# A DLRM tower on one core: MLP layers in 64-row matmul pieces over two PSUM banks, ScalarE's sums straight to SBUF, and one PSUM copy moved to ScalarE

## The reference

```python
e = stack([tbl_f[ids[:, f]] for f in range(32)], axis=1)      # 1024 x 32 x 64
p, q = e[:, ROW_IDX], e[:, COL_IDX]                           # the 496 pairs i < j
z = einsum('bne,hne,bnh->bn', p, kernel, q)                   # kernel: 64 x 496 x 64
h = concatenate([z, dense_ctx], axis=1)                       # 1024 x 512
h = maximum(h @ W_top1 + b_top1, 0)                           # 512 -> 512
h = maximum(h @ W_top2 + b_top2, 0)                           # 512 -> 256
y = h @ W_top3                                                # 256 -> 1
```

## Time and profile before

| | |
|---|---|
| median of 3 runs | 402.61 us (401.84 to 402.92) |
| the profiled execution | 402.61 us, its span 400.8 us |
| TensorE matmul busy | 371.6 us, 93% of the span |
| VectorE busy | 354.9 us, 89% |
| ScalarE busy | 315.4 us, 79% |
| GpSimd busy | 241.8 us, 60% |
| mean granted TensorE clock | 0.987 |

### The profile page before, as it was taken

How to read it: one execution, slowest core, us unless ns; L and a number is a source line. 1 busy time by engine, 2 the same in 40 slices (tenths; PEclk the granted TensorE clock), 3 DMA queues, 4 the chain that set the end, 5 groups by cost and what they waited for, 6 DMA issues and landing times.

```text
span 400.8 us, 13206 instructions
## 1 busy us (share of the span) xinstructions
PE 371.6 (93%) x4464; PEld 277.7 (69%) x4464; DVE 354.9 (89%) x512; ACT 315.4 (79%) x2887; POOL 241.8 (60%) x260
## 2 busy tenths in 40 slices
PE   0468889899999999999999999999999999999987
PEld 0244657587777877678777877778777877778666
DVE  0249999899999999999999999999999999999971
ACT  1157696897969987898869987798869988798862
POOL 5677777766666666676676666666666666640000
PEclk9968999999999999999999999999999999999999
DMA  3566792111111111111111111111111111110000
GB/s 82 173 196 198 226 262 41 26 27 24 26 26 24 25 25 27 23 28 26 25 27 24 25 25 24 29 25 26 24 25 26 25 28 23 25 21 3 2 2 2
DMA packets 14563, 19.25 MB, mean 48 GB/s; under 512 B 7192, under 2 KB 7840, under 8 KB 14496
## 3 DMA queue, kind: packets, MB, share of 16 engines
q0 software_dynamic: 8192, 8.40, 11.2%
q1 hardware_dynamic: 6304, 10.00, 7.9%
HBM read 18.39 MB, written 0.00 MB: 46 GB/s over the span
## 4 chain that ended last, share of the span: by engine, by line
PE 84%; DVE 5%; POOL 4%; issue 3%; DMA 2%; ACT 1%; DVEq 0%
PE u_ps L570 28%; PE u_ps L577 26%; PE side_ps L591 14%; PE side_ps L625 7%; POOL emb L363 4%; PE side_ps L636 3%; PE u_ps L555 2%; DVE prod_s L502 2%; DVE prod_t L484 2%; DMA emb<-tbl,ids_sb 2%; ACT prod_s L404 1%; PE u_ps L657 1%; PE side_ps L649 1%; PE side_ps L617 1%; DVE emb_t L471 1%
## 5 line engine op out<-in xcount | busy, mean ns | idle before, releaser
L404 ACT ACTIVATE prod_s<-prod_s 128x64 f32<-128x64 f32 x1408 | 293.0, 372 | 77.1 <-DVE prod_s L502 76.6
L363 POOL DMA_INDIRECT emb<-tbl,ids_sb x256 | 241.6, 944 | 114.6 <-issue 35.4
L404 ACT ACTIVATION_READ_ACCUMULATOR prod_s<-prod_s 128x1 f32 x1408 | 277.2, 287 | 0.0
L484 DVE TENSOR_TENSOR prod_t<-u_ps,emb_t 128x1024 f32<-128x1024 f32 x128 | 155.7, 1217 | 8.0 <-PE u_ps L570 7.3
L502 DVE TENSOR_TENSOR prod_s<-u_ps,emb 128x512 f32<-128x512 f32 (+4 forms) x224 | 151.2, 721 | 11.1 <-PE u_ps L577 10.5
L570 PEld LDWEIGHTS u_ps<-emb_t,k_sb 64*128 64x128 f32 x2048 | 129.2, 190 | 36.8 <-DVE prod_s L502 12.8
L570 PE MATMUL u_ps<-emb_t,k_sb 64*128 64x128 f32 x2048 | 139.5, 279 | 3.3 <-DVE emb_t L471 1.5
L577 PE MATMUL u_ps<-k_sb,emb_t 64*128 64x512 f32 (+5 forms) x704 | 128.0, 483 | 3.7 <-DVE emb_t L471 2.1
L577 PEld LDWEIGHTS u_ps<-k_sb,emb_t 64*128 64x128 f32 x704 | 63.2, 192 | 26.9 <-issue 11.3
L591 PE MATMUL side_ps<-prod_t,pick_sb 128*32 128x256 f32 x1024 | 63.3, 382 | 0.0
L511 DVE TENSOR_REDUCE h<-prod_s 128x4 f32<-128x256 f32 x128 | 52.4, 409 | 0.0
(11 more groups left out here) (23 smaller groups left out, 38.3 us busy)
## 6 DMA issues: line engine op xcount, KB each, us to landing
k_sb<-k_pairs SPq DMA_DIRECT2D x9, 512.0 KB, 4.0
emb<-tbl,ids_sb POOLq DMA_INDIRECT x256, 2.5
k_sb<-k_pairs SPq DMA_DIRECT2D x6, 480.0 KB, 4.6
w_sb<-w SPq DMA_DIRECT2D x1, 1024.0 KB
w_sb<-w SPq DMA_DIRECT2D x1, 512.0 KB
k_sb<-k_pairs SPq DMA_DIRECT2D x1, 448.0 KB, 3.9
h<-dense SPq DMA_DIRECT2D x8, 8.0 KB
out<-y_row SPq DMA_DIRECT2D x8, 0.5 KB
```

Source lines behind the costliest of these rows:

```text
L363: nc.gpsimd.indirect_dma_start(emb[t % EMBS][:, f * EMBED:(f + 1) * EMBED], None, tables[f], bass.IndirectOffsetOnAxis(ap=ids_sb[:, t, f:f ...
L404: done = nc.scalar.activation(slot, slot, ACT.Copy, accum_out=acc_ps[:, t % 2, column:column + 1])
L484: done = nc.vector.tensor_tensor(prod_t[at % TRING][:].rearrange("p (h x) -> p h x", h=HALVES), u, low.unsqueeze(1).to_broadcast([P, HALVE ...
```

## The change

Five things are edited together.

1. **The hidden layers in 64-row pieces.** `layer` does half of the work of a pair of outputs in one piece: row half 0 of the array works on one output, row half 1 on the other, with two different banks (`side_ps` and the new `hidden_ps`), over the four chunks of the input. The second piece (phase 1) swaps the halves and so completes both sums; it waits until the first piece is complete. The first layer is four pieces after blocks 7, 9, 10 and 12, the second layer two after blocks 17 and 18.
2. **Sums straight to SBUF.** ScalarE's `accum_out` points to `h0[t]` in SBUF. `acc_ps` and `copy_acc` go; its bank becomes `hidden_ps`.
3. **Part 0 is copied by ScalarE.** For tiles 2 to 7 the copy of the turned part 0 is done by ScalarE (at 26 in its order, so between its sums of blocks 25 and 27), with a semaphore of its own, `emb_turned`.
4. **Positions.** Turns after blocks 4 and 11 instead of 3 and 12; `late_spread` after block 4 instead of 3, with five picks instead of four; ScalarE's `copy_spread` stands after its sums of block 1 instead of 2; `hidden1`'s relu after 12 (at 13), as before behind the sums of block 10; the logit and picks 0 to 3 after block 22 instead of 23, three picks after block 31 instead of four; the logit is copied at 30 instead of 23.
5. **Gathers.** The entries that waited for MLP steps wait for blocks 12, 18 and 8. The order string is written as one string and is the same.

```diff
-    ("u", 9), ("u", 10), ("u", 12), ("mlp", 2), ("u", 13), ("u", 14), ("u", 15), ("u", 17), ("u", 18), ("mlp", 3),
+    ("u", 9), ("u", 10), ("u", 12), ("u", 12), ("u", 13), ("u", 14), ("u", 15), ("u", 17), ("u", 18), ("u", 18),
...
-    ("u", 0), ("u", 1), ("u", 3), ("pick", 15), ("u", 4), ("u", 5), ("u", 6), ("u", 8), ("mlp", 0)]
+    ("u", 0), ("u", 1), ("u", 3), ("pick", 15), ("u", 4), ("u", 5), ("u", 6), ("u", 8), ("u", 8)]
...
-TURN_AT = {3: 1, 12: 2}
+TURN_AT = {4: 1, 11: 2}
...
+COPY_EARLY_AT = 26
+
+def on_act(kind, t, part):
+
+    return kind == "turn" and t > 1 and part == 0
...
-PORTION = NT // 4
-LATE_SPREAD_AT, HIDDEN1_AT, LATE_HIDDEN1_AT, HIDDEN2_AT, SUMS_AT, LATE_SUMS_AT, SPREAD_AT = 3, 8, 12, 18, 23, 27, 31
-LAST_SPREAD_AT = 29
+LATE_SPREAD_AT, SPREAD_COPY_AT = 4, 1
+PORTIONS = {22: (0, 4), 27: (4, 8), 31: (8, 11)}
+LAST_PORTIONS = {22: (0, 4), 27: (4, 8), 29: (8, 11)}
+SUMS_AT = min(PORTIONS)
+LATE = max(stop for _, stop in PORTIONS.values())
+LOGIT_COPY_AT = 30
+HIDDEN1 = {7: (0, 0), 9: (0, 1), 10: (1, 0), 12: (1, 1)}
+HIDDEN2 = {17: 0, 18: 1}
+HIDDEN1_COPY_AT, HIDDEN2_COPY_AT = 13, 18
...
-        acc_ps = ctx.enter_context(nc.psum_tensor("acc_ps", [P, 2, 2 * P], F32))
+        hidden_ps = ctx.enter_context(nc.psum_tensor("hidden_ps", [P, 4, P], F32))
+        mlp_ps = [side_ps, hidden_ps]
...
-                    done = nc.scalar.activation(slot, slot, ACT.Copy, accum_out=acc_ps[:, t % 2, column:column + 1])
+                    done = nc.scalar.activation(slot, slot, ACT.Copy, accum_out=h0[t][:, column:column + 1])
...
-            def copy_acc(t):
-                act.wait_ge(summed_a, (t + 1) * NS)
-                nc.scalar.activation(h0[t][:, :ON_ACT], acc_ps[:, t % 2, :ON_ACT], ACT.Copy).then_inc(acc_copied, 1)
+            def copy_turned(t, part):
+                act.wait_ge(slot_filled, filled("turn", t, part))
+                first, last = parts_of(t)[part]
+
+                at = SLOT_USE["turn", t, part]
+                turned_half = u_ps[at % USLOTS][:].rearrange("p (h m b) -> p m h b", h=HALVES, b=P // 2)
+                nc.scalar.activation(emb_t[t % 2][:, first:last, :].rearrange("p m (h b) -> p m h b", h=HALVES),
+                                     turned_half[:, :last - first], ACT.Copy).then_inc(emb_turned, 1)
...
+            def layer(to, weights, x, phase, m0, m1):
+
+                for c in range(4):
+                    for half, m in enumerate((m1, m0) if phase else (m0, m1)):
+                        rows = slice(half * P // 2, (half + 1) * P // 2)
+                        done = nc.tensor.matmul(to[m], weights[rows, c, m * P:(m + 1) * P], x[rows, c],
+                                                start=(phase == 0 and c == 0), stop=(phase == 1 and c == 3))
+                return done
+
+            def hidden1(t, pair, phase):
+                part = 2 * pair + phase
+                if part == 0:
                     pe.wait_ge(side_copied, STEPS * t + 1)
...
+                else:
+                    pe.wait_ge(layer_part, LAYER_PARTS * t + part)
+                to = [mlp_ps[m // 2][:, m % 2] for m in range(4)]
+                layer(to, w1_sb, h0_t, phase, pair, pair + 2).then_inc(mlp_mm if part == 3 else layer_part, 1)
+
+            def hidden2(t, phase):
+                if phase == 0:
+                    pe.wait_ge(side_copied, STEPS * t + 2)
+                else:
+                    pe.wait_ge(layer_part, LAYER_PARTS * (t + 1))
+                layer([mlp_ps[m][:, 0] for m in range(2)], w2_sb, h1_t, phase, 0, 1,
+                      ).then_inc(mlp_mm if phase else layer_part, 1)
...
-            pick_sums(last, 3 * PORTION, NT - 1)
+            pick_sums(last, LATE, NT - 1)
+            pe.wait_ge(y_copied, last)
             spread_straight(last, spread_ps).then_inc(last_turned, 1)
```

More of the change, by code:

```diff
@@ L233, in slot_uses, with filled, turn_of @@
     return uses
-SLOT_USE = {use: at for at, use in enumerate(slot_uses())}
-def used(t, n):
[L241 to L249, removed]
-PORTION = NT // 4
-LATE_SPREAD_AT, HIDDEN1_AT, LATE_HIDDEN1_AT, HIDDEN2_AT, SUMS_AT, LATE_SUMS_AT, SPREAD_AT = 3, 8, 12, 18, 23, 27, 31
-LAST_SPREAD_AT = 29
-PICKS_AT = [SUMS_AT, LATE_SUMS_AT, SPREAD_AT, LATE_SPREAD_AT]
-MLP_STEPS_AT = [HIDDEN1_AT, HIDDEN1_AT, LATE_HIDDEN1_AT, HIDDEN2_AT]
+SLOT_USES = slot_uses()
+SLOT_USE = {use: at for at, use in enumerate(SLOT_USES)}
+COPY_EARLY_AT = 26
+def on_act(kind, t, part):
+    return kind == "turn" and t > 1 and part == 0
+EMPTIED = {}
+for use in SLOT_USES:
+    EMPTIED[use] = 1 + sum(on_act(*other) == on_act(*use) for other in EMPTIED)
+def filled(kind, t, at):
+    return SLOT_USE[kind, t, at] + 1
+def used(t, n):
+    return EMPTIED["u", t, n]
+def turn_of(t, n):
+    return "turn", t, part_of(parts_of(t), n)
+assert all(SLOT_USE[turn_of(t, n)] < SLOT_USE["u", t, n] for t in range(TILES) for n in range(NB))
+LATE_SPREAD_AT, SPREAD_COPY_AT = 4, 1
[7 more added lines that the diff above has]
+HIDDEN1_COPY_AT, HIDDEN2_COPY_AT = 13, 18
 STEPS = 3
-LOGIT = CHUNKS - 1
+LOGIT = 3
+LAYER_PARTS = 4
 def build(nc, ids, tables, k_pairs, dense, w1, b1, w2, b2, w3, ident, pick, out):
@@ L466, in copy_turned @@
                 at = SLOT_USE["turn", t, part]
-                dve.wait_ge(slot_filled, at + 1)
+                dve.wait_ge(slot_filled, filled("turn", t, part))
                 first, last = parts_of(t)[part]
@@ L521, in _ @@
                         copy_turned(t, own_turns(t)[n])
-                    if early_turn(t, n):
+                    if early_turn(t, n) and not on_act("turn", t + 1, 0):
                         copy_turned(t + 1, 0)
@@ L537, in _, with emptied @@
         def _(pe):
+            def emptied(use):
+                pe.wait_ge(emb_turned if on_act(*use) else slot_emptied, EMPTIED[use])
             def slot_free(at):
                 if at >= USLOTS:
-                    pe.wait_ge(slot_emptied, at - USLOTS + 1)
+                    emptied(SLOT_USES[at - USLOTS])
                 return u_ps[at % USLOTS]
@@ L560, in block_u @@
             def block_u(t, n):
-                pe.wait_ge(slot_emptied, turned(t, n))
+                emptied(turn_of(t, n))
                 u = slot_free(SLOT_USE["u", t, n])
@@ L618, in spread_straight @@
                 return done
-            def hidden1(t, portion):
-                if portion == 0:
-                    pe.wait_ge(side_copied, STEPS * t + 1)
-                for m in range(2 * portion, 2 * portion + 2):
-                    for c in range(4):
-                        done = nc.tensor.matmul(side_ps[:, m], w1_sb[:, c, m * P:(m + 1) * P], h0_t[:, c],
-                                                start=(c == 0), stop=(c == 3))
-                    if m == 3:
-                        done.then_inc(mlp_mm, 1)
-                    else:
-                        done.then_inc(mlp_step, 1)
@@ L632, in hidden2 @@
-            def hidden2(t):
-                pe.wait_ge(side_copied, STEPS * t + 2)
-                for m in range(2):
-                    for c in range(4):
-                        done = nc.tensor.matmul(side_ps[:, m], w2_sb[:, c, m * P:(m + 1) * P], h1_t[:, c],
-                                                start=(c == 0), stop=(c == 3))
-                    if m == 1:
-                        done.then_inc(mlp_mm, 1)
-                    else:
-                        done.then_inc(mlp_step, 1)
+            def layer(to, weights, x, phase, m0, m1):
[5 more added lines that the diff above has]
+                return done
```

77 lines of the change are left out of this document (31 added, 46 removed).

## The result

The changed kernel took 415.48 us, median of four runs (412.62 to 416.56), against 402.62 us (401.84 to 402.92) for the kernel before on the same chip: 1.031 times as long, 95% interval 1.026 to 1.037. The forecast was 393.8 us and faster. Its profiled execution took 415.1 us, its span is 413.3.

A forecast was written before the change was run, and what follows sets the result against it. TensorE was taken to bound the 45.39 us tile period, VectorE only 1.27 us behind. Six tiles at 1.20 us plus 2.0 at the end, less 0.4 of new waits, saves 8.8: 402.6 to 393.8 us, range 391 to 400.

The forecast's parts named there:

- Sums straight to SBUF: ScalarE's 176 sums a tile: SBUF adds at most 0.06 us a pair, taken as 0, so still 0.197 us.
- The first rival: ScalarE's sums get slower, TensorE waits for the relu before the second layer: 406 us at 30 ns, 426 at 60; chance 0.11.
- 68e: Delay of the relu before the second layer if each of 68 sums ahead costs e ns more a pair.
- The break-even of 22 ns: Extra per ScalarE pair at which TensorE's wait before the second layer, 1.2 us, eats the gain of a tile.
- The pieces: Hidden layers on TensorE: two 64-row pieces at 0.89 us replace a 2.18 us group, saving 0.40 us each, 1.20 a tile.
- The copy of part 0: Moving it takes 1.14 us a tile off VectorE and costs ScalarE 1.0 us, hidden with 0.6 us to spare.
- The gather's margin: GpSimd's last gather of a tile lands at 15.9 us, before the turn at 16.1 to 16.3: 0.3 us against 3.5.
- The relu's margin: ScalarE's relus end at 23.1 us, TensorE wants them for the second layer at 23.4: 0.3 us against 2.7 before.
- The end: Last tile: three groups save 1.20 us, one pick less 0.47, dropping `copy_acc` 0.33; together 2.0 us.

The follow-up runs named there:

- the kernel with fewer sums: The changed kernel with ScalarE leaving out two sums in each straight block, 144 pairs a tile instead of 176: 393.32 us, ratio 0.977 to the kernel before.
- five slots on VectorE: The changed kernel with VectorE summing five slots of each straight block instead of four, ScalarE 160 pairs a tile instead of 176: 398.11 us, ratio 0.989.
- the second set: One of six sets of experiment runs, each beside the kernel before on the same chip; here the kernel before took 402.6 us.
- run 16: Not a follow-up run: "run" is a verb here, the accumulating 64-row matmuls run 16 records in 0.88 us.
- in the first: Set of experiment runs on another chip, where the kernel before took 459.0 us; the changed kernel with 32 sums a tile left out had ratio 1.021.

## Why the prediction was wrong, by its own steps

**The step that failed** is "Sums straight to SBUF", where it says "I take 0". The bound beside it held: at most 0.06 us a pair, and 0.041 was measured. The reason for taking the low end failed: that the read's end lies under the next ACTIVATE says nothing of what paces the starts. The rows of before had only sums written to PSUM, where the reads' ends could fall 0.46 us behind (0.61 - 0.15) at no cost to the starts; with the sum in SBUF each start comes 0.041 us later. The upper bound was read from the first pair of a run, whose records are the shortest of the run; that it held is in part luck. The Trainium skill, "ScalarE: Activation LUTs", in its section on the steps of an ACTIVATE, calls PSUM the lower-latency destination. The traces agree for the pace of the pairs, 0.197 us to PSUM and 0.239 to SBUF, and for the read at a run's start, 0.15 us and 0.19; the read's mean length is the other way round, 287 ns in the kernel before and 189 in the changed one.

**The first rival came true, in its mechanism and nearly in its size.** With 68e = 2.8 us and 0.3 us free it gives 2.5 us of wait a tile. The relus give 0.57 us back (1.02 us instead of 1.59), which leaves 1.9; TensorE's matmuls stood for 1.87 us, and the period grew by 2.2 (46.35 - 44.15). The break-even of 22 ns lies below the 41. By its sum 402.6 + 7 x (46.35 - 45.39) - 0.8 = 408.5 us. Its chance of 0.11 was too low: by the row the extra was unknown between 0 and 60 ns, and above 22 ns the kernel is slower, so nearly two thirds of the unknown lay on the slow side.

**What no rival had** is the clock. I left it out because nothing left TensorE idle, and the rival that makes it idle took no account of it either. Four tiles of six lost 1.6 us more, 6.5 us together: 408.5 + 6.5 = 415.0 us, and 415.1 was measured in the profiled execution. The mean clocks of the four runs differ (0.967 to 0.988), so the number of such tiles probably differs too; only this run has a trace.

**The pieces**: right. 0.88 us for 16 records, the blocks behind them at their usual price, a saving of at least 0.40 us a group; the halves overlap when they accumulate.

**The copy of part 0**: right in its costs. VectorE's work fell to 42.96 us (42.98), ScalarE's copy takes 999 ns on the page (1.0 forecast), and TensorE waits for it in no steady tile of the kernel with fewer sums. What VectorE's relief is worth by itself was only tried on the other chips, where it made no difference (1.019 to 1.024 against 1.021).

**The gather's margin** held: with fewer sums TensorE is busy for 44.15 of 44.15 us. **The relu's margin** of 0.3 us was about right: with 56 pairs at 0.239 us, which is the forecast's 13.4 us, the relus end 0.8 us early, 0.57 of it by being shorter, so by this estimate some 0.2 us would be left with the relus at 1.59.

**The end**: the hand-over from ScalarE's last sum to TensorE is 0.14 us where before had 0.49, as forecast, but the 20 records ahead of it take 2.51 us instead of 2.17.

```profile
401.08 2.51 ACT prod_s L430 x20
403.59 0.14 issue
```

Outside the six tiles the changed kernel takes 128.7 us of its span (413.3 - 284.6), the wait for the relus in the last tile included, and the kernel before 128.5 (400.8 - 272.3): of the 2.0 us that the forecast gains there nothing is left.

The forecast's 393.8 us is what the kernel with fewer sums took (393.32), though that kernel has 0.8 us of slack at the relus where the forecast had counted 0.3, and less to sum at the end.

**What stays open**: whether a later second layer helps the changed kernel where the kernel before takes 402.6 us; five slots on VectorE together with a layer one block later there; what the pauses on the other chips are; what in ScalarE paces the pairs; and why the clock fell in four tiles behind the wait for the relus and not in a fifth with the same wait.

## What to carry to other kernels

Where a cost is bounded between nothing and a small number, multiply both ends by the count on the path first: 0.06 us was harmless for one pair and 4 us for the 68 that stand ahead of the relus. Take an instruction's price from start to start over a long run, not from the lengths of its records: in the kernel before a read's grew from 0.15 to 0.61 us while the starts kept their pace, and that an end overlaps the next instruction doesn't say what paces the starts. And before an engine's slack in one place (2.7 us at the relus here) is spent on moving work, ask what that slack was covering, and when an edit brings a new TensorE wait, look at the granted clock behind it: here waits of 1.9 us cost another 1.6 us four times in five.

## What the runs showed of the hardware

A 64-column ACTIVATE with its sum costs 0.239 us with the sum in SBUF and 0.197 with it in PSUM; this held in both kernels and at three loads of ScalarE. With the sum in PSUM the recorded lengths of ACTIVATE and read grow along an unbroken run of 56 pairs (0.26 to 0.70 and 0.15 to 0.61 us) while the starts stay 0.197 us apart, and the four relus behind take 1.59 us; with the sum in SBUF the lengths stay (0.24 and 0.19) and the relus take 1.02. Behind a TensorE wait of 1.85 to 1.87 us, the granted clock was 1.2 GHz for some 3.4 us in four tiles and stayed at 2.4 GHz in one; behind waits of 1.43 us, and of 0.7 us a tile with five slots on VectorE, it stayed at 2.4 GHz. Accumulating 64-row matmuls into two banks run 16 records in 0.88 us, and a 128-row group among 64-row blocks costs 0.44 us more than two such pieces. The same program took 402.6 us in the result's and the second set's runs and 459 to 468 us on four other chips, with pauses inside unbroken TensorE groups and waits of VectorE for a releaser that the profile doesn't know, and an edit that gave 2.3% in the second set cost 2.1% in the first.
